# A graph network kernel: matmuls that nobody reads, in both attention loops, and another order of loads in the counted stage

## What is computed

```python
# additive attention: 4 heads of 32 channels
projected = (x @ W).reshape(N, 4, 32)
src, dst = projected[row], projected[col]
scores = einsum("ehc,hc->eh", tanh(src + dst), att)
scores = exp(scores - max(scores, axis=0))
out = segment_sum(src * scores[:, :, None], col) / maximum(segment_sum(scores, col), 1e-12)

# GAT: 2 heads of 128 channels
e = leaky_relu(xl[src] + xr[dst], 0.2)
alpha = segment_softmax(einsum("ehd,hd->eh", e, att), dst)
out = segment_sum(xl[src] * alpha[..., None], dst).mean(axis=1)
```

## Time and profile before

| | us |
|---|---|
| median of three runs | 4942.16 (4939.04 to 4942.38) |
| span of the profiled execution, first to last instruction | 4898.1 |
| around it (median less span) | 44.1 |
| additive loop, window in the span | 680 to 1920 |
| GAT loop, window in the span | 2065 to 3350 |

### The profile page before, as it was taken

One profiled execution on the slowest core, in us unless ns is written; L12 is line 12 of the kernel. 1 busy time (PEld: TensorE's weight loads), 2 busy tenths in 40 slices (PEclk: granted clock), 3 DMA queues, 4 the chain that ended last, 5 costly groups with the idle time before them and its releaser, 6 DMA issues. The chain is left out here.

```text
span 4898.1 us, 89702 instructions
## 1 busy us (share of the span) xinstructions
PE 3999.0 (82%) x22566; PEld 2260.3 (46%) x22566; DVE 2847.4 (58%) x8457; ACT 1737.4 (35%) x4474; POOL 2828.1 (58%) x3060
## 2 busy tenths in 40 slices
PE   3997927788887877488888888885399999999987
PEld 1344414445544544344444444442256655556652
DVE  7994032333333334555555555556678888888868
ACT  3773023344344334333333333331322222222227
POOL 0122356666666663555555555554368888888862
PEclk8998957776777777688988888886699999999999
DMA  2333422222222221333333333330056666666650
GB/s 80 91 87 103 147 71 57 57 56 57 57 56 57 56 57 27 113 98 96 97 97 96 96 97 96 97 96 18 21 97 104 105 105 104 104 105 104 104 110 13
DMA packets 377425, 402.41 MB, mean 82 GB/s; under 512 B 86457, under 2 KB 322502, under 8 KB 377030
## 3 DMA queue, kind: packets, MB, share of 16 engines
q0 software_dynamic: 151904, 198.72, 21.0%
q1 hardware_dynamic: 225382, 202.21, 14.4%
HBM read 312.91 MB, written 87.78 MB: 82 GB/s over the span
## 5 line engine op out<-in xcount | busy, mean ns | idle before, releaser
L897 POOL DMA_INDIRECT gathered<-table,sources x952 | 903.6, 949 | 600.6 <-issue 259.9
L1709 POOL DMA_INDIRECT sums<-gathered,idx x606 | 988.7, 1632 | 217.8 <-issue 166.4
L1571 PE MATMUL bank<-wide 128*128 128x512 bf16 x3636 | 851.5, 379 | 0.0
L2228 DVE TENSOR_REDUCE neg_raw<-bank 80x1 f32<-80x512 f32 (+1 forms) x404 | 276.6, 685 | 725.9 <-remote 252.1
L897 POOL DMA_INDIRECT wide<-table,sources x464 | 438.7, 946 | 275.1 <-issue 125.7
L1571 PEld LDWEIGHTS bank<-wide 128*128 128x128 bf16 x3636 | 347.7, 98 | 364.1 <-issue 1.7
L2178 ACT ACTIVATE msg<-bank,neg_top 80x512 f32<-80x512 f32 (+1 forms) x404 | 275.7, 682 | 643.1 <-DVE neg_top L2230 353.6
L1222 POOL TENSOR_TENSOR acc<-acc,msg 128x20 f32 x404 | 108.3, 268 | 411.2 <-issue 244.6
L2221 DVE TENSOR_TENSOR zact<-zact,bank 128x512 f32<-128x512 f32 x404 | 259.5, 683 | 123.1 <-ACT zact L2170 72.9
L2106 PE MATMUL bank<-zact,att_cells 128*32 128x512 f32 x808 | 289.4, 732 | 37.9 <-issue 36.2
L2088 PEld LDWEIGHTS bank<-ident,gathered 128*128 128x128 f32 x1360 | 191.8, 165 | 258.0 <-issue 232.2
(11 more groups left out here) (406 smaller groups left out, 7603.9 us busy)
## 6 DMA issues: line engine op xcount, KB each, us to landing
zact<-in_src_flat SPq DMA_DIRECT2D x202, 192.0 KB
edge_rows<-in_attr_rows SPq DMA_DIRECT2D x202, 128.0 KB
dst_pair<-local_rows SPq DMA_DIRECT2D x177, 128.0 KB
gathered<-table,sources POOLq DMA_INDIRECT x952
dst_pair<-local_rows SPq DMA_DIRECT2D x202, 64.0 KB
counts<-wide SPq DMA_DIRECT2D x4, 3000.0 KB
counts<-fm_ab SPq DMA_DIRECT2D x4, 3000.0 KB
fm_ab<-counts SPq DMA_DIRECT2D x4, 3000.0 KB, 11.0
```

Of the source, the lines that this page charges most:

```text
L897: pool.indirect_dma_start(out=g[:, j, :], out_offset=None, in_=table, in_offset=bass.IndirectOffsetOnAxis(ap=mine, axis=0)).then_inc(rows_ ...
L1571: pe.matmul(k.bank[b][:, :], k.split[t.two][:, c, :], k.source_hot[t.two][:, b * CHUNK:(b + 1) * CHUNK], start=first, stop=c == PARTS - 1, ...
L1709: pool.indirect_dma_start(out=k.sums[j], out_offset=bass.IndirectOffsetOnAxis(ap=k.idx[t.slot][:, j:j + 1], axis=0), in_=out_rows(t)[:, j, ...
L2228: dve.tensor_reduce(raw, score_bank(t), AX.X, ALU.max, negate=True).then_inc(top_found, 1)
```

## The change

It has three parts.

- In `sums` of the additive loop the wait for `kept` comes first, then a semaphore increment and four matmuls (`WARM1`) of 128 rows by 432 columns, f16, from `iota_c` into columns 80 to 511 of the bank whose columns 0 to 79 the sums are about to fill; then the wait for the weights and the sums as before.
- In `turn_sums` of GAT likewise: the wait for `kept`, an increment, two matmuls (`WARM2`) of 448 columns into columns 64 to 511 of bank 7, then the wait for `copied` and the transpose as before. Nothing reads these columns.
- In the counted stage the waits against the register's value are gone. Only the first two thirds are loaded ahead of the rebuilding rounds; TensorE waits in the round for the first of them, SP for the second; the last third is loaded after the rounds. TensorE waits for constants.

```diff
--- before.py
+++ after.py
@@ -59,6 +59,8 @@
 HEADS2 = 2
 STRIDE1 = WIN
 STRIDE2 = 32
+WARM1 = 4
+WARM2 = 2
 
 
 def ceil_div(a, b):
@@ -1354,6 +1356,7 @@
             hot_ready, counted, evicted, stored, free = (st.sem("hot_ready"), st.sem("counted"), st.sem("evicted"),
                                                          st.sem("stored"), st.sem("free"))
             loaded, begun = [st.sem(f"loaded{i}") for i in range(2)], [st.sem(f"begun{i}") for i in range(3)]
+            second_there, rounds_done = st.sem("second_there"), st.sem("rounds_done")
             summed, kept, adds_begun, added = st.sem("summed"), st.sem("kept"), st.sem("adds_begun"), st.sem("added")
             thirds = [(i * GROUP // 3, (i + 1) * GROUP // 3) for i in range(3)]
 
@@ -1367,18 +1370,26 @@
                 @block.sync
                 def _(sp):
                     sp.sem_inc(free, 1)
-                    for landed in begun:
+                    for landed in begun[0:2]:
                         sp.sem_inc(landed, 16)
+
+                    def load_third(i):
+                        lo, hi = thirds[i]
+                        sp.dma_start(k.counts[0][:, lo:hi, :], k.all_counts[lo:hi, :, :].rearrange(
+                            "t p c -> p t c")).then_inc(begun[i], 16)
                     with sp.Fori(0, k.rebuild) as n:
-                        for (lo, hi), landed in zip(thirds, begun):
-                            sp.wait_ge(landed, n * 16 + 16)
-                            sp.dma_start(k.counts[0][:, lo:hi, :], k.all_counts[lo:hi, :, :].rearrange(
-                                "t p c -> p t c")).then_inc(landed, 16)
+                        for i in range(2):
+                            sp.wait_ge(begun[i], n * 16 + 16)
+                            load_third(i)
                         sp.wait_ge(evicted, n + 1)
                         sp.dma_start(k.all_counts[bass.ds(tile(n), 1), :, :].rearrange("t p c -> (t p) c"),
                                      again).then_inc(stored, 16)
                         sp.wait_ge(stored, n * 16 + 16)
                         sp.sem_inc(free, 1)
+                        sp.wait_ge(begun[1], n * 16 + 32)
+                        sp.sem_inc(rounds_done, 1)
+                    sp.sem_inc(second_there, 1)
+                    load_third(2)
 
                     def load(now):
                         if now is None:
@@ -1409,6 +1420,7 @@
                     with pe.Fori(0, k.rebuild) as n:
                         pe.wait_ge(hot_ready, n + 1)
                         cell_counts(k, pe, 0, k.bank[0]).then_inc(counted, 1)
+                        pe.wait_ge(begun[0], n * 16 + 32)
 
                     def sums(now):
                         if now is None:
@@ -1416,8 +1428,10 @@
                         pe.wait_ge(loaded[now.par], (now.pair + 1) * 16)
                         wait_count(pe, kept, now.g - 1)
                         for i, (lo, hi) in enumerate(thirds if first(now) else [(0, now.size)]):
-                            if first(now):
-                                pe.wait_ge(begun[i], k.rebuild * 16 + 16)
+                            if first(now) and i == 1:
+                                pe.wait_ge(second_there, 1)
+                            if first(now) and i == 2:
+                                pe.wait_ge(begun[2], 16)
                             for b in range(k.blocks):
                                 mm = block_sums(k, pe, parts, now, b, lo, hi)
                         mm.then_inc(summed, 1)
@@ -2128,9 +2142,18 @@
                     pe.matmul(top_bank(t), a.own[lanes(t), :], k.top_cells[lanes(t), :], start=True,
                               stop=True).then_inc(top_turned, 1)
 
+                def keep_warm(bank, free, count):
+
+                    for _ in range(count):
+                        pe.matmul(bank[:, free:CHUNK], k.iota_c[:, 0:P], k.iota_c[:, 0:CHUNK - free], start=True,
+                                  stop=True)
+
                 def sums(t):
+                    wait_count(pe, copied if gat else kept, t.t if gat else t.t - 1)
+                    if not gat:
+                        pe.sem_inc(turns_begun, 1)
+                        keep_warm(k.bank[6 + t.two], cells, WARM1)
                     pe.wait_ge(weight_ready, t.t + 1)
-                    wait_count(pe, copied if gat else kept, t.t if gat else t.t - 1)
                     if merge:
                         merge.finish_spreads(pe, t)
                     g = rows(t)
@@ -2146,8 +2169,10 @@
                     mm.then_inc(sums_ready, 1)
 
                 def turn_sums(t):
+                    wait_count(pe, kept, t.t)
+                    pe.sem_inc(turns_begun, 1)
+                    keep_warm(k.bank[7], cells, WARM2)
                     pe.wait_ge(copied, t.t + 1)
-                    wait_count(pe, kept, t.t)
                     pe.sem_inc(turns_begun, 1)
                     pe.transpose(turned_bank(t), k.tile_rows[t.two][:, :],
                                  k.ident[0:cells, 0:cells]).then_inc(sums_turned, 1)
```

## The result

The changed kernel takes 4965.7 us (median, 4964.6 to 4968.2) where the kernel before, run beside it, takes 4941.9 (4939.0 to 4942.4). The ratio is 1.0048, with an interval of 1.0036 to 1.0059: **24 us slower**, where I had forecast 61 us faster.

A forecast was written before the change was run, and what follows sets the result against it. TensorE was taken to bound the additive loop at the lower clock level, something else at the upper. Additive -48, GAT -10 and counted stage -3 made -61 us: 4942 to 4881 us, range 4790 to 5030.

The forecast's parts named there:

- The bound at the lower clock level: Additive loop: TensorE bounds a tile at 6.55 us at the lower level, something else at 5.6 at the upper; -48 us.
- my formula: Additive loop with the added matmuls: a tile costs 8.0 x + 5.6 (1 - x), x the share at the lower level.
- Three counts: Additive tile at the upper level: 4.6 us by TensorE's steps, 5.8 by POOL, 6.8 by VectorE's maxima; 5.6 taken.
- The clock: Additive loop: mean granted clock rises from 0.73 to 0.92, leaving 16% of the time at the lower level.
- The cover of the additive matmuls: Additive loop, upper level: four matmuls cost 0.8 us a tile, covered by the 2.0 us TensorE has to spare.
- The cover in GAT: GAT: two matmuls (0.4 us upper, 0.7 lower) mostly covered by the 0.60 us wait before the transpose; -10 us.
- wrong in its kind: Named failure case: the new matmuls lengthen a tile at the upper level, where the prediction held them covered.
- The counted stage: Counted stage: the small store lands 3 to 4 us sooner, first sums begin 3 us sooner; -3 us taken.
- The base: Whole kernel: profiled span 4898.1 us, median 4942.2; the 44.1 us around the span are left alone by the change.
- The handoff is the bound at both levels: Both loops: a tile stays at 6.12 us (additive) and 6.43 (GAT) whatever the clock; 4939 us, chance 0.15.
- The clock stays low: Both loops: other waits keep the clock down and uncovered matmuls cost 1.45 us an additive tile; 5025 us, chance 0.27.
- Up throughout: Both loops: no additive tile at the lower level, 5.6 us each, -105 us, GAT -26; 4808 us, chance 0.20.

The follow-up runs named there:

- s2: Changed kernel with only the additive loop's four added matmuls a tile, none in GAT, on chip C; ratio 1.0011 to the kernel before.
- s1: Changed kernel with no added matmuls in either loop (moved waits, increments and new load order stay), on chip C; ratio 1.0005 to the kernel before.
- e1: Changed kernel with no added matmuls in either loop (moved waits, increments and new load order stay), on chip A; ratio 0.9997 to the kernel before.
- s3: Changed kernel with only GAT's two added matmuls a tile, none in the additive loop, on chip C; ratio 1.0035 to the kernel before.
- a3: Changed kernel with only the additive loop's four added matmuls a tile, none in GAT, on chip A; ratio 0.9988 to the kernel before.
- a5: The whole change, four added matmuls a tile in the additive loop and two in GAT, on chip D; ratio 1.0046 to the kernel before.
- e10: Changed kernel without added matmuls, two of four gathers a tile left out beyond the first 12 or 8 tiles, chip D; 4087 us, before 4906.
- e3: Changed kernel with only GAT's two added matmuls a tile, none in the additive loop, on chip A; ratio 1.0027 to the kernel before.
- e6: Changed kernel without added matmuls, gathering only the first 12 (additive) or 8 (GAT) tiles' rows, on chip B; ratio 0.8263 to the kernel before.
- e11: Changed kernel without added matmuls, all attention-loop gathers replaced by plain copies of the same size, on chip D; 4003 us, before 4906.

## Why the prediction was wrong, step by step

**The bound at the lower clock level: this step failed, and the sum with it.** I held that at the lower level TensorE is the bound (6.55 us a tile) and at the upper level something quicker (5.6), and counted 48 us for the shift between them. s2 against s1 makes this shift on one chip and gains nothing. Sorting the 201 steps of TensorE by the clock granted in each shows why. In s1 55 steps lie at the lower level (a mean clock under 0.6; 7.27 us each), 73 are mixed (7.49) and 73 lie at the upper (over 0.9; 3.98). In s2 only 19 lie at the lower (now 9.46), 53 are mixed (8.32) and 129 at the upper (4.81). Both lists add up to 1240 us. The slow steps weren't slow because the clock was low; the clock was low where TensorE had stood waiting, and with the matmuls the same waits stand in fewer, longer steps. The count by level above is the direct test: without added matmuls a tile takes 5.96 us at the lower level by GpSimd's count and 6.59 at the upper, where I had 6.55 and 5.6. I read a price from stretches picked by their clock, and so took the mark of the wait for its cause. That my formula gives 6.2 us at the measured clock is luck: neither of its two prices was seen.

**The earlier trace rows had told it.** Three counts contradicted each other, and by VectorE's maxima, one for each finished tile, tiles came no faster at the upper level. I explained it away by TensorE running ahead, which was true, and then averaged instead of asking what a loop that runs ahead is waiting for. GpSimd's count at the lower level, which I left out, is 320.8 / (199.38 / 3.78) = 6.1 us a tile: with VectorE's 5.9 that made two counts against the 6.55. The pace of a loop is to be counted on the engine at its end.

**The clock.** 0.92 was forecast for the additive loop, 0.85 came (0.84 on chip C, 0.98 on chip A, where the waits are short). The mechanism held: a fill in the wait raises the clock.

**The cover of the additive matmuls** held: 3.6 us on chip C, nothing on chip A, where even eight found room. Their price at the upper level was 0.69 us a packed step, where I had 0.8.

**The cover in GAT failed.** I set 0.4 us of matmuls against a wait of 0.60. The price was too small: a packed step grows from 4.45 to 5.08 us. On chip A that alone explains the loss, since a tile had 5.00 - 4.45 = 0.55 us to spare and got 0.63: 0.08 us over, 16 us in 201 steps (17 measured). And the cover was a mean over tiles, where the sum needs it tile by tile: on chip C a step takes 6.5 us in the mean and has room, but the quick ones have none. This is the case that I had named as wrong in its kind, new matmuls lengthening a tile at the upper level, and it came true in GAT, not where I looked for it. The loss of 14 to 17 us lies within the bounds of +40 and -26 that I gave, on the other side of the -10 that I took.

**The counted stage.** First sums 2.6 us sooner, 3 to 4 forecast; s1 and e1, which have this part and the moved waits alone, show no difference in time (1.0005 and 0.9997).

**The base.** "44.1 us around the span" was no work around it: spans lie about 2 us under their times, so the profile was of a quicker execution. It left the forecast as it was, since I added to the median, but it is part of why the two profiles show +27 and +40 in the loops where one chip shows +4 and +13.

**The sum of the parts.** Against before: s1 +0.05%, the additive matmuls +0.06% on it (s2 - s1), GAT's +0.30% (s3 - s1): +0.41% (some 20 us), where the whole was measured at +0.48% (0.36 to 0.59) and, on chip D, at +0.46% (0.29 to 0.62).

**The rivals.** "The handoff is the bound at both levels" (4939 us) was right for the additive loop, down to VectorE's count and the "remote" waits, and had 0.15; its sign of a clock near 1.0 did not come (0.85), and it lacked GAT's loss. "The clock stays low" (5025) lies on the measured side, and two of its signs came, a clock of 0.75 to 0.85 and longer waits of GpSimd; but it wanted TensorE near 100% busy, and after shows 978 of 1200 us. The Trainium skill, page "TensorE: Matmul & The Clock Gate", section "HAM oscillation — how this bites in real kernels", had it that interrupted matmul work goes cold again at each wait. The granted clock of 0.84 in s2 bears that out. What no run here bears out is that a warmer clock gains time in such a loop. "Up throughout" (4808) asked for a clock of 1.0: on chip A a3 had 0.98, and gained 0.12%.

No version is better on both kinds of chip: the additive matmuls alone give 0.9988 (0.9979 to 0.9996) on chip A and 1.0011 (1.0002 to 1.0020) on chip C, both hardly clear of no change.

## What to carry to other kernels

Before paying for a higher TensorE clock, count what the last engine of the loop finishes per microsecond in stretches at either clock level. If the counts agree, the clock is a symptom of the wait, and lifting it moves the wait to the next engine. Price added work by the packed step of the engine that gets it, with and without, and not by its columns; and hold the packed step against the pace and against the quickest tiles, not against a mean wait. In GAT on chip A the pace was 5.00 us and the packed step went from 4.45 to 5.08.

## What the runs showed of the hardware

**Chips differ by 12 to 13% on this kernel**, 4381 against 4906 to 4942 us, with the same durations of single instructions (a gather 0.95 us, a maximum 0.685 us, on both). All of it lies in the two attention loops. What differs is the time from TensorE's last matmul to the engine that waits for it: in the additive loop 3.5 us in the mean on chip C (s1), 0.12 on chip A (e1); in GAT 3.2 against 0.07. One pair of rows of each, first e1 (sums end at 2306.98 + 1.07 = 2308.05, the copy starts 0.04 us later), then after (2704.83 + 1.07 = 2705.90, the copy 2.83 us later):

```profile
2306.98 1.07 PE L2163 MATMUL bank<-h_nm,edge_rows 128*32 128x128 f32 x16
...
2308.09 0.26 ACT L2209 COPY tile_rows<-bank 64x128 f32<-64x128 f32 x1 [0.23 <-PE bank L2163]
```
```profile
2704.83 1.07 PE L2163 MATMUL bank<-wide,edge_rows 128*32 128x128 f32 x16
...
2708.73 0.26 ACT L2209 COPY tile_rows<-bank 64x128 f32<-64x128 f32 x1 [2.16 <-DMA wide<-table,sources]
```

**On the late chips it needs GpSimd's gathers at full rate**: in the additive loop 0.26 us without gathers, 0.53 with half of them, 0.24 with plain copies, over 3 with all. Gathers thus cost more than their 0.95 us there. The Trainium skill, page "DMA: Bandwidth & Descriptors", section "SWDGE vs HWDGE vs iDMA", puts plain and indirect transfers issued from GpSimd on one path; here they differ in their issue time (0.54 and 0.95 us) and in what they do to others.

**The late traces also lack records.** In the additive loop the traces of s1, a5, before and after hold only 60 to 63% of the signals of TensorE, VectorE and ScalarE, and e10's 71%; those of e1, e3, e6 and e11 hold 99 to 100%. So gathers at a high rate on such a chip go with missing records as well as with late signals. Whether the recording of a trace has a part in the lateness isn't known: every timed execution here has its span and clock on record. Why one chip shows none of it, and what holds the signals back, no run here tells.
